# Early-fusion block (patch tokens, attention, switch feed-forward): batch loop reordered on all engines, table mean in four slots

## The reference

```python
h = patches(x) @ proj_w.T + proj_b + pos_embed          # 8 batches x 36 tokens x 192
h = concatenate([h, txt], axis=1)                       # 8 x 164 x 192
# attention, 12 heads, on xn = layernorm(layernorm(h)) * ln_w
avg_wte = mean(wte, axis=0)                             # table of 50257 x 192
Q = xn[:, None] * W_qk[None, :, None, :]                # one vector of weights per head
attn = softmax(causal(Q @ Q.T / sqrt(192)))
out = attn @ (xn - avg_wte) * (1 / position)
h = h + concat_heads(out) @ W_o.T                       # 12 * 192 -> 192
# switch feed-forward: 16 experts, capacity 64 per batch and expert
h = h + switch_moe(layernorm(h), ln_w, w_router, wi, wo)
```

## Time and profile before

| what | us |
|---|---|
| median of 3 runs | 372.57 |
| the profiled execution's own time | 372.14 |
| its span, first to last instruction | 370.4 |
| start to `z_transpose` of turn 0 | 37.84 |
| turn 0 | 30.91 |
| turns 1 to 5, together | 130.65 |
| from turn 6 to the first feed-forward block | 86.2 |
| feed-forward blocks and end | 84.8 |

### The profile page before, as it was taken

One profiled execution on the slowest core, in us unless ns is written; L12 is line 12 of the kernel. 1 busy time (PEld: TensorE's weight loads), 2 busy tenths in 40 slices (PEclk: granted clock), 3 DMA queues, 4 the chain that ended last, 5 costly groups with the idle time before them and its releaser, 6 DMA issues.

```text
span 370.4 us, 6796 instructions
## 1 busy us (share of the span) xinstructions
PE 332.7 (90%) x2352; PEld 306.4 (83%) x2352; DVE 219.9 (59%) x546; ACT 127.9 (35%) x438; POOL 169.0 (46%) x181
## 2 busy tenths in 40 slices
PE   5886779999799899899899898999949999999992
PEld 1866679989699799799798798999824999999991
DVE  1479638678669679578588888656476222222221
ACT  2065423644643453454436004545720111111110
POOL 3067375583574763862953501450562134444321
PEclk9899889999999999999999999999998999999997
DMA  7399999899799899799797999900223599999930
GB/s 226 114 419 341 215 213 212 236 177 210 221 196 213 225 199 239 191 199 271 162 198 155 295 229 237 230 11 0 84 101 93 165 276 276 273 265 272 273 93 15
DMA packets 20176, 74.29 MB, mean 201 GB/s; under 512 B 3388, under 2 KB 9021, under 8 KB 18874
## 3 DMA queue, kind: packets, MB, share of 16 engines
q0 software_dynamic: 7344, 30.57, 40.8%
q1 hardware_dynamic: 9898, 40.40, 36.8%
q10 hardware_dynamic: 2912, 3.04, 2.9%
HBM read 66.12 MB, written 9.25 MB: 203 GB/s over the span
## 4 chain that ended last, share of the span: by engine, by line
PE 39%; issue 18%; DMA 14%; POOL 14%; DVE 8%; ACT 3%; POOLq 1%; SPq 0%; DVEq 0%; ACTq 0%
PE bO L1198 18%; DMA wbuf<-in_wte 11%; PE bE L1198 10%; PE bS L1198 5%; PE bJ L1198 4%; POOL AwA L390 4%; DMA H<-in_txtA 4%; POOL PA L416 3%; POOL wbuf L401 3%; POOL AwB L390 2%; ACT PA L552 2%; POOL PB L416 1%; DVE negmax L791 1%; PE bT L1544 1%; DVE PTB0L L808 1%
## 5 line engine op out<-in xcount | busy, mean ns | idle before, releaser
L552 ACT ACTIVATE PA<-bS,negmax 128x128 f32<-128x128 f32 x96 | 33.9, 366 | 85.2 <-DVE negmax L791 85.2
L416 POOL TENSOR_TENSOR PA<-PA,rn 128x512 f32<-128x512 f32 x24 | 25.8, 1075 | 64.3 <-DVE rn L803 64.3
L390 POOL TENSOR_TENSOR AwA<-zT,w 96x512 f32<-96x512 f32 x45 | 53.4, 1514 | 3.3 <-ACT zT L534 3.3
L1198 PE MATMUL bJ<-wo_sb,oTA 128*128 128x192 f32 x288 | 51.4, 328 | 0.0
L1198 PEld LDWEIGHTS bS<-zT,AwA 96*128 96x128 f32 x384 | 48.0, 197 | 1.1
L1198 PE MATMUL bS<-zT,AwA 96*128 96x128 f32 x384 | 48.2, 280 | 0.0
L1198 PEld LDWEIGHTS bJ<-wo_sb,oTA 128*128 128x128 f32 x288 | 46.2, 190 | 0.0
L1198 PE MATMUL bO<-PA,wx 96*128 96x112 f32 x384 | 45.4, 275 | 0.5 <-DVE PA L1171 0.5
L1198 PEld LDWEIGHTS bO<-PA,wx 96*128 96x128 f32 x384 | 44.9, 192 | 0.7 <-DVE PA L1171 0.7
L463 POOL DMA_INDIRECT out<-PA,yrow x16 | 15.0, 940 | 56.1 <-DVE PA L1187 56.1
L689 ACT ACTIVATE AwA<-bO 128x448 f32<-128x448 f32 x16 | 8.7, 543 | 78.4 <-PE bO L1198 52.8
(11 more groups left out here) (247 smaller groups left out, 690.9 us busy)
## 6 DMA issues: line engine op xcount, KB each, us to landing
wbuf<-in_wte POOLq DMA_DIRECT2D x20, 1344.0 KB, 13.0
wx<-in_wi SPq DMA_DIRECT2D x16, 576.0 KB
wx<-in_wo SPq DMA_DIRECT2D x16, 576.0 KB
wx<-in_wte SPq DMA_DIRECT2D x6, 1344.0 KB, 8.5
dispatched<-zeros SPq DMA_DIRECT2D x7, 675.5 KB, 10.3
wbuf<-in_wte SPq DMA_DIRECT2D x2, 1344.0 KB, 12.1
AwA<-dispatched ACTq DMA_DIRECT2D x14, 168.9 KB
wo_sb<-in_wo_attn SPq DMA_DIRECT2D x1, 1728.0 KB, 6.9
```

Of the source, the lines that this page charges most:

```text
L390: nc.gpsimd.tensor_tensor(o, zT[:, k, ss].unsqueeze(1).to_broadcast(list(o.shape)), w2[:, k, hs].unsqueeze(2).to_broadcast(list(o.shape)), ...
L416: nc.gpsimd.tensor_tensor(t, t, q.unsqueeze(2).to_broadcast(list(t.shape)), ALU.mult).then_inc(p_ready, 1)
L552: last = nc.scalar.activation(PA[:, h, :], bank[:, j * SA:(j + 1) * SA], ACT.Exp, bias=negmax[:, h:h + 1], accum_out=lsum[:, h:h + 1])
L1198: return nc.tensor.matmul(o, l, r, start=start, stop=stop, skip_group_check=True)
```

## The change

On ScalarE `zt_copy` stands ahead of the exponentials of rounds 3 and 4, and `t_copy(b, 3)` ahead of `exps(b + 1, (0,))`. On GpSimd the first group of `weigh` is the first thing of a turn, ahead of `normalise(b, 3..4)`; the adds stand behind `weigh` groups. On TensorE `p_transpose(b, 2)` stands ahead of `value(b, 0)`. The table has four slots (two in `wbuf`, and `wx[2]`, `wx[3]`), so 4 chunks are loaded and 18 added: two in the prologue, 16 over turns 0 to 5. Plain chunks come in two halves with a semaphore each. The slots are added to each other by `tensor_tensor` on whole rows. All expert weights are loaded after `acc_ready`. In the prologue the inputs of the embedding come in two halves, batches 0 and 1 are embedded straight into token rows, statistics are taken batch by batch, the text rows are loaded as 80 and 12 partitions, `hB` is loaded last of ScalarE's early loads, and the filler matmuls around `z_transpose(0, 0)` are gone. The conversion of `mat` on ScalarE moves from behind turn 1 to turn 6. Statistics and factors of batches 2 to 7 move into turn 0.

```diff
-WBUF = 2
+WBUF = 4
...
+        wchunk = [wbuf[:, 0:WR * EMB], wbuf[:, WR * EMB:2 * WR * EMB], wx[2][:, :], wx[3][:, :]]
...
-        plain = wx[0][:, :]
-        psums = wx[1][:, 0:WPLAIN * EMB]
+        HALF = WR // 2 * EMB
+        plain = [wx[0][:, h * HALF:(h + 1) * HALF] for h in range(2)]
+        psums = wx[1][:, 0:2 * WPLAIN * EMB]
-        wfold = wx[1][:, WPLAIN * EMB:(WPLAIN + 1) * EMB]
...
         def _(sp):
             def plain_loads(sp):
 
+                sp.wait_ge(tok_ready, 5)
                 for n in range(WPLAIN):
-                    if n:
-                        sp.wait_ge(plain_used, 4 * n)
-                    sp.dma_start(plain, wv[:, WCHUNKS - WPLAIN + n, :]).then_inc(plain_in, 16)
-
-            sp.dma_start(pw_sb, projw).then_inc(pat_in, 16)
-            sp.dma_start(pat_sb, patches).then_inc(pat_in, 16)
-            sp.dma_start(H[IMG:128, 0:NBATCH, :], txtA).then_inc(txt_in, 16)
+                    for h in range(2):
+                        if n:
+                            sp.wait_ge(plain_used, 4 * n - 2 + 2 * h)
+                        sp.dma_start(plain[h], wv[:, WCHUNKS - WPLAIN + n, h * HALF:(h + 1) * HALF]).then_inc(plain_in[h], 16)
+
+            for part, arrived in ((slice(0, 3), pat_in), (slice(3, 6), pat2_in)):
+                sp.dma_start(pw_sb[:, part, :], projw[:, part, :]).then_inc(arrived, 16)
+                sp.dma_start(pat_sb[:, part, :], patches[:, part, :]).then_inc(arrived, 16)
+
+            for p0, p1 in ((IMG, 116), (116, 128)):
+                sp.dma_start(H[p0:p1, 0:NBATCH, :], txtA[p0 - IMG:p1 - IMG]).then_inc(txt_in, 16)
+            sp.dma_start(H[0:BP, NBATCH:SLOTS, :], txtBp).then_inc(late_in, 16)
...
-            sp.wait_ge(txt_in, 16)
+            sp.wait_ge(w_in, 32)
+            sp.wait_ge(txt_in, 32)
+            for s in range(2):
+                sp.dma_start(wchunk[s], wv[:, s, :]).then_inc(wte_first[s], 16)
             sp.dma_start(wo_sb[:, :, :], wo_attn).then_inc(wo_in, 16)
-            for s in range(WBUF):
-                sp.dma_start(wchunk[s], wv[:, s, :]).then_inc(wte_first, 16)
-            sp.dma_start(H[0:BP, NBATCH:SLOTS, :], txtBp).then_inc(late_in, 16)
+            for s in range(2, WBUF):
+                sp.dma_start(wchunk[s], wv[:, s, :]).then_inc(wte_first[s], 16)
             sp.dma_start(cst2[:], cst2_d[:, 0:C_MAT]).then_inc(cst2_in, 16)
             sp.dma_start(wtail[:], wte[VOCAB - WTAIL:VOCAB, :]).then_inc(wtail_in, 16)
 
+            plain_loads(sp)
...
-            for q in range(2, NSLOT):
-                weights(q, q)
             sp.wait_ge(acc_ready, 1)
-            for q in range(2):
+            for q in range(NSLOT):
...
-            rsqrt(rstd[:, :, 0:2], nmr[:, :, 0:2], 1)
+            for b in range(2):
+                rsqrt(rstd[:, :, b:b + 1], nmr[:, :, b:b + 1], b + 1)
...
-            def add_wte(c, s, before):
-
-                if is0(before):
-                    pool.wait_ge(wte_first, 16 * WBUF)
+            def add_wte(c):
+
+                s, before = c % WBUF, c // WBUF
+                if before == 1:
+                    pool.wait_ge(wte_first[s], 16)
                 else:
-                    pool.wait_ge(wte_in[s], 16 * before)
-                    pool.sem_inc(pool_seq, 1)
-                pool.dma_start(wchunk[s], wv[:, ds(c, 1), :].rearrange("p c x -> p (c x)"), accum_op=ALU.add,
+                    pool.wait_ge(wte_in[s], 16 * (before - 1))
+                pool.dma_start(wchunk[s], wv[:, c, :], accum_op=ALU.add,
                                max_dma_last_dim=WR * EMB * 4 // 2).then_inc(wte_in[s], 16)
-
-            def add_wte_nth(i, r):
-
-                add_wte(6 * i + r + WBUF, r % 2, 3 * i + r // 2)
...
             pool.wait_ge(w2_ready, 1)
-            weigh(0, 1, (1,), range(3))
-            rsqrt(rstd[:, :, 2:NBATCH], nmr[:, :, 2:NBATCH], 2)
-            weigh(0, 1, (1,), (3,))
-            normalise(0, range(1))
-            add_wte(2, 0, 0)
-            normalise(0, range(1, 2))
-            add_wte(3, 1, 0)
-            normalise(0, range(2, 3))
-
-            def iteration(b, i, r):
-
+            weigh(0, 1, (1,))
+            add_wte(WBUF)
+            add_wte(WBUF + 1)
+            normalise(0, range(3))
+
+            def iteration(b, chunks=()):
+
+                n = t_before(b, "z") + 1
+                weigh(b + 1, n, (0, 1), (0,))
                 normalise(b, range(3, SPR))
-                for k in range(4):
-                    if r is not None and k < 3:
-                        add_wte_nth(i, r + k)
-                    if k == 0:
-                        weigh(b + 1, t_before(b, "z") + 1, (0, 1), (0, 1))
-                    elif k == 1:
-                        weigh(b + 1, t_before(b, "z") + 1, (0, 1), (2,))
-                        normalise(b + 1, (0,))
-                    elif k == 2:
-                        normalise(b + 1, (1,))
-                        weigh(b + 1, t_before(b, "z") + 1, (0, 1), (3,))
-                    else:
-                        normalise(b + 1, (2,))
+                weigh(b + 1, n, (0, 1), (1,))
+                for c in chunks[0:1]:
+                    add_wte(c)
+                weigh(b + 1, n, (0, 1), (2,))
+                normalise(b + 1, (0,))
+                if is0(b):
+                    rsqrt(rstd[:, :, 2:NBATCH], nmr[:, :, 2:NBATCH], 3)
+                for c in chunks[1:2]:
+                    add_wte(c)
+                normalise(b + 1, (1,))
+                weigh(b + 1, n, (0, 1), (3,))
+                for c in chunks[2:3]:
+                    add_wte(c)
+                normalise(b + 1, (2,))
...
+            for b in range(NBATCH - 2):
+                iteration(b, range(WBUF + 2 + 16 * b // 6, WBUF + 2 + 16 * (b + 1) // 6))
+            iteration(NBATCH - 2)
...
-            act.dma_start(hB[:], txtB).then_inc(hb_in, 16)
+            for dst, src in ((w2[:], wqk), (ln96[:], lnw)):
+                act.dma_start(dst, src).then_inc(w_in, 16)
             for dst, src in ((posb, pos), (pbb, projb)):
                 act.dma_start(dst, src).then_inc(pos_in, 16)
-            for dst, src in ((w2[:], wqk), (ln96[:], lnw)):
-                act.dma_start(dst, src).then_inc(w_in, 16)
+            act.dma_start(hB[:], txtB).then_inc(hb_in, 16)
...
             def iteration(b, more=True):
                 t_copy(b, 0)
                 t_copy(b, 1)
-                exps(b, range(3, SPR))
                 if more:
                     zt_copy(t_before(b, "z") + 1, 1)
+                exps(b, range(3, SPR))
                 o_copy(b, 0)
                 t_copy(b, 2)
                 o_copy(b, 1)
                 o_copy(b, 2)
+                t_copy(b, 3)
                 if more:
                     exps(b + 1, (0,))
-                t_copy(b, 3)
                 t_copy(b, 4)
...
-            iteration(1)
-
-            act.wait_ge(mat_in, 16)
-            nc.scalar.activation(mat[:, :, :].rearrange("p m s -> p (m s)"), mat32, ACT.Copy).then_inc(mat_ready, 1)
-            with act.Fori(2, LAST - 1) as b:
+            with act.Fori(1, LAST - 1) as b:
...
+            dve.wait_ge(txt_in, 32)
+            for b in range(2):
+                add_patches(b)
+                row_sums(b, b + 1)
+                variances(b, b + 1)
...
+            def slot_add(s, t):
+
+                for w in (s, t):
+                    dve.wait_ge(wte_in[w], slot_loads(w))
+                for r in (0, WR // 2):
+                    a, b = (chunk_rows(wchunk[w], r, r + WR // 2) for w in (s, t))
+                    last = nc.vector.tensor_tensor(a, a, b, ALU.add)
+                link(last)
+
+            def table_total():
 
                 dve.wait_ge(plain_used, 4 * WPLAIN)
                 dve.wait_ge(wtail_in, 16)
-                link(nc.vector.tensor_reduce(wsum[:, :], psums.rearrange("p (n e) -> p e n", e=EMB), X, ALU.add))
-                link(nc.vector.tensor_tensor(wsum[0:WTAIL, :], wsum[0:WTAIL, :], wtail[:, :], ALU.add))
-
-            def slot_total(s):
-
-                dve.wait_ge(wte_in[s], 16 * ((WCHUNKS - WPLAIN) // WBUF - 1))
-                for k in range(2):
-                    q = slice(k * EMB // 2, (k + 1) * EMB // 2)
-                    last = nc.vector.tensor_reduce(wfold[:, q], wchunk[s].rearrange("p (r e) -> p e r", e=EMB)[:, q, :], X, ALU.add)
-                link(last)
-                last = nc.vector.tensor_tensor(wsum[:, :], wsum[:, :], wfold[:, :], ALU.add)
-                if s == WBUF - 1:
-                    last.then_inc(acc_ready, 1)
-                else:
-                    link(last)
+                w, p = wchunk[0], psums
+                link(nc.vector.tensor_tensor(chunk_rows(p, 0, 6), chunk_rows(p, 0, 6), chunk_rows(p, 6, 12), ALU.add))
+                nc.vector.tensor_tensor(chunk_rows(p, 0, 3), chunk_rows(p, 0, 3), chunk_rows(p, 3, 6), ALU.add)
+                link(nc.vector.tensor_tensor(chunk_rows(w, 0, 7), chunk_rows(w, 0, 7), chunk_rows(w, 7, 14), ALU.add))
```

(42 more changed lines are left out.)

135 lines of the change are left out of this document (67 added, 68 removed).

## The result

The changed kernel takes 367.69 us (median of 4 runs, 367.48 to 368.43) against 372.61 us for the one before on the same chip (370.71 to 373.33), a ratio of 0.9881 with a 95% interval of 0.9858 to 0.9903. That is 4.9 us less; 11.6 were forecast. Its profiled execution takes 367.87 us, the span is 366.0.

What follows compares the result with a forecast made beforehand. TensorE was taken to set a turn's length, with the DMA engines close behind. From 372.1, minus 4.2 (prologue), 4.8 (turn 0) and 5.6 (turns 1 to 5), plus 3.2 (turn 6), gave 360.7, stated as 361 us; range 354 to 369.5.

Steps and rivals of the forecast that it cites:

- rival (2): Turn 6: additions at the price of reductions or behind GpSimd, costing 10 instead of 3.2; 367.5 us, chance 0.07.
- Turn 0: First turn of the loop: shrinks to 26.1 us from 30.9, a gain of 4.8 us.
- some 0.3 us for statistics: Turn 0: what it was to take beyond the length of turn 1, 0.3 us.
- plain sums of the same 672 elements: Plain sums on VectorE: listed among the parts of the change that cost nothing.
- rival (3): Turn 0: late first loads or plain half hold GpSimd or VectorE as before; 365.5 us, chance 0.07.
- Prologue: Before turn 0: earlier text, z(0) at 16.9 and smaller pieces behind it, a gain of 4.2 us.
- The text's landing: Prologue: text rows land near 12.5 instead of 15.67, 3.2 us earlier.
- rival (5): Prologue and turn 0: without fillers the clock stays low, up to 15 us lost; 376 us, chance 0.04.
- Turns 1 to 5: Loop: TensorE's waits for AwA and the B rows' low part go, a gain of 5.6 us.
- Turn 6: Last turn: the table's sum by whole-row additions takes longer, a loss of 3.2 us.
- the 1 us for GpSimd: Turn 6: 1 us added because GpSimd still weighs while the first additions run.

Runs made afterwards that it cites:

- e9: Changed kernel with GpSimd's first two adds issued behind the weighing of group 1 in turn 0 instead of in the prologue: 365.19 us, ratio 0.9806.
- e2: Changed kernel with the first load of slot 3 issued behind the first two plain halves: 365.63 us, ratio 0.9843.
- e1: Changed kernel with the plain sums of turn 0 moved behind row maxima of batch 1 on VectorE: 364.71 us, ratio 0.9766.
- e10: Changed kernel with hB early, first adds late, turn 0's plain sums and variances later, wr_sb's product in the prologue, 12 fillers in turn 6: 359.27 us.
- e13: Changed kernel with the text rows loaded by one DMA of 92 partitions instead of two of 80 and 12: 374.01 us in one run.
- e3: Changed kernel with 18 filler products on TensorE ahead of z_transpose(0, 0): 367.64 us, ratio 0.9887.
- e5: Kernel of e4 with GpSimd's first two adds issued behind the weighing of group 1 in turn 0: 359.06 us in one run.
- e6: Changed kernel with the edits of e1, e2 and e4 and 14 fillers instead of the 18 of e3: 367.66 us, ratio 0.9851.
- e12: Changed kernel with GpSimd again normalising rounds 3 and 4 and issuing an add ahead of its first weighing: 376.39 us in one run.
- e4: Changed kernel with hB loaded second on ScalarE's queue instead of last: 371.49 us, ratio 1.0001.
- e7: Kernel of e6 with turn 0's variances behind t_low(0, 3) and the product of wr_sb in the prologue: 366.42 us, ratio 0.9854.

## Why the prediction was wrong

Direction, range (354 to 369.5) and mechanism of the loop were right; the likeliest value was 6.7 us too low. All four terms were off by more than 1 us, turn 0 by 4.5. That 367.69 lies beside rival (2)'s 367.5 is chance: the additions of turn 6 did not come at the price of reductions (3.03 us for 2688 elements, 1.13 ns each).

- **Turn 0 (-4.8, found -0.3) is the step that failed,** in two places. The first is the landing of the plain half: "Issued from 12.5 on, slot 2 (5.9 MB) lands near 32, slot 3 (7.3 MB) near 36, the first plain half (8 MB) near 39 ... That leaves 5 us or more." The loads were issued at 12.44 and slot 2 landed near 28.6, but the half landed at 47.8. The rate of 0.31 MB per us was that of the kernel before, whose first adds go out at 31.36 and 33.34, so that they ran beside the loads only for the last third of the way to 39.3; the changed kernel puts them out at 24.88, and they are about twice as dear per MB. The sum took the adds in by the rate of that kernel, and not by when they go out and what they cost. With those adds late the half lands at 35.4 (e9), sooner than forecast.
- The second is what stands on VectorE ahead of it: "some 0.3 us for statistics", and "plain sums of the same 672 elements" at nothing. The work of the sums is the same, but in turn 0 two of them (2.47 us) and the variances of six batches (0.50 and 2.63 us, the latter beside GpSimd's weighing) stand ahead of low parts that TensorE waits for. Of TensorE's 3.65 us these cost 2.09 and the wait for the half 1.56 (e2); with the sums behind, 0.84 are left (e1).
- In steps of turn 0: 30.59 as changed, 28.92 without the wait (e2), 27.02 when the adds are late and the long instruction is short too (e9), 25.90 with sums and variances behind the low parts (e10), just under the 26.1 of the forecast. It is rival (3), given 0.07. Its 365.5 had turn 0 right; what is missing to 367.7 lies in the prologue (2.2) and turn 6 (1.5), less what the loop gave more (1.2).
- **Prologue (-4.2, found -2.0).** The text's landing (12.5) was exact, and that the split makes it is shown by e13. By the Trainium skill, "DMA: Bandwidth & Descriptors", section "Why a DMA increments its semaphore by 16 and not by 1", 92 partitions use 4 engines and the new pieces 16 and 12; e13's 2.93 us agree with it. (Had the landing stayed, the sum would have been 360.7 + 3.2 = 363.9, not 363.7.) `z(0)` came 1.35 us later than forecast (18.25 for 16.9), and the stretch from there to turn 0 took 17.6 us where 16.7 were taken. "`hB` ... may hold VectorE a little" was too small: `z_transpose(0, 0)` comes at 17.65 in the mean of the eight executions with `hB` early (16.98 to 18.10) and at 18.73 in the eight with it late and the text in two (17.89 to 19.58), 1.1 us. Behind it stands the clock after the 4.81 us of idle time: 16.88 us from `z_transpose(0, 0)` to turn 0, 14.6 in e3 and also in e5, e6 and e13, more than the whole of what this stretch is too long. It is rival (5) in small; the sum had no term for it. The idle time alone does not tell it: in e13, behind 3.06 us of it, the second half of the embedding took 2.35 us and the stretch 14.6 without any fillers.
- **Turns 1 to 5 (-5.6, found -6.8)** were right in cause (e12) and low in size: besides `AwA` and the B rows' low part the 0.31 us for `PTAL` went too. That the DMA engines would stay under the turn's length was not so in three of the turns (above), without a cost.
- **Turn 6 (+3.2, found +4.7).** The sum ended 3.6 us later into the turn, 3.7 with GpSimd's part were forecast; the pair of additions beside GpSimd's weighing takes 3.93 us, the others 3.03, so the 1 us for GpSimd was right. The clock behind TensorE's new wait was not in the sum: 0.9 to 2.5 us by the executions above, 2.5 in the one against which the 4.7 are read. That is more than the miss of 1.5, so the forecast of what the later sum itself costs TensorE was about 1 us too high.

The errors of turn 0 and of the prologue hang together, which the sum could not show: a prologue that is 2 us shorter gives nothing or loses while the bytes set turn 0 (e3, e4), and 12 us come at once when they don't (e5, one run).

## What to carry to other kernels

When the DMA engines are full, as here from 15 to 55 us, the landing of a load was set by the bytes issued ahead of it and beside it, not by the consumer's order: count them by queue, with accumulating DMAs at their own price, and issue late what is wanted late. A stretch made shorter ahead of such a wait was worth nothing until the wait was gone, so test its cure together with the cure of the wait. Moving an instruction moves what runs beside it, too: look in the trace at what the other engines do then, before the whole gain is put down to one cause. And look at the duration of the products behind a wait of TensorE: here the lower clock behind waits of 4.81 and 2.67 us cost up to 2.3 and 2.5 us.

## What the runs showed that was not expected

- An accumulating DMA to the slots took 15.0% of the engines' time per MB, a plain load 7.7% (12 to 45 us, above; 7.5 in e9, without adds); before the change 14.9 (1.97 MB, 29.4%) and 8.0 (7.51 MB, 60.2%).
- A `tensor_scalar` of 12 columns on VectorE takes 0.17 us when GpSimd does not work beside it (e7), 0.80 when it issues adds (e9) and 2.63 us when it weighs (changed kernel); it has one tensor input only. In the prologue three instructions of 2 columns took 0.96 to 0.99 us each while GpSimd weighed.
- A filler loop or an order that puts due work into the wait gave the same time up to `value(6, 3)` in turn 6 (31.01 and 31.02 us).
